# A graph-attention layer and a gated feed-forward layer on one core: the turned one-hots of the targets move from VectorE to ScalarE, made from single bytes

## The reference, cut to what matters

```python
x = x + gnn(layernorm(x), edges)
x = x + ffn(layernorm(x))

def gnn(x, edge_index, W, att_src, att_dst, bias):
    xp = (x @ W).reshape(n, 4, 64)
    a_src, a_dst = ...                      # a number per node and head
    alpha = leaky_relu(a_src[src] + a_dst[dst])
    ex = exp(alpha - segment_max(alpha, dst)[dst])
    w = ex / segment_sum(ex, dst)[dst]
    out = segment_sum(xp[src] * w[..., None], dst).reshape(n, 256) + bias
    return elu(out)

def ffn(x, ...):                            # 256 -> 1024 -> 256 with gelu,
    ...                                     # added for the half of the nodes with the largest router weight
```

## Time and profile before

| | us |
|---|---|
| timed: median of 3 runs (lowest, highest) | 2208.46 (2207.24, 2212.64) |
| profiled execution: span from its first to its last instruction | 2573.5 |
| of it: up to the first gathers, main stage, the rest | 132, 2350, 91.5 |

### The profile page before, as it was taken

How to read it: one execution, slowest core, us unless ns; L and a number is a source line. 1 busy time by engine, 2 the same in 40 slices (tenths; PEclk the granted TensorE clock), 3 DMA queues, 4 the chain that set the end, 5 groups by cost and what they waited for, 6 DMA issues and landing times.

```text
span 2573.5 us, 29095 instructions
## 1 busy us (share of the span) xinstructions
PE 1981.2 (77%) x9511; PEld 1633.8 (63%) x9512; DVE 1581.4 (61%) x3510; ACT 744.5 (29%) x1478; POOL 1554.5 (60%) x1626
## 2 busy tenths in 40 slices
PE   8935877877877877878778877877777777877787
PEld 6723666666666666666666666666666666666666
DVE  4555655665655655656656665666665665666576
ACT  4512222222322222322232232232232232223223
POOL 2366666666666666666666666666666666666630
PEclk9967988888888889889888888988988988889889
DMA  8844444444444444444444444444444444444447
GB/s 287 276 143 121 123 134 124 132 138 120 137 138 118 132 135 124 135 140 120 134 137 128 130 136 124 134 134 130 128 134 131 127 139 124 131 136 136 119 159 312
DMA packets 157137, 369.12 MB, mean 143 GB/s; under 512 B 46646, under 2 KB 73682, under 8 KB 155699
## 3 DMA queue, kind: packets, MB, share of 16 engines
q0 software_dynamic: 75088, 208.19, 30.1%
q1 hardware_dynamic: 74706, 145.62, 16.9%
q10 hardware_dynamic: 7184, 13.41, 1.4%
HBM read 328.20 MB, written 38.89 MB: 143 GB/s over the span
## 4 chain that ended last, share of the span: by engine, by line
POOL 38%; issue 23%; PE 19%; another core or an unknown queue 9%; DVE 3%; DMA 3%; ACT 2%; POOLq 1%; DVEq 0%; SPq 0%; ACTq 0%
POOL rows L692 38%; PE ag_ps L1057 7%; PE h_ps L1021 4%; PE ag_ps L934 3%; PE y_ps L1040 3%; DMA rows<-node_rows,ends 3%; POOLq L402 1%; DVE oh L1366 1%; DVE rows L1404 1%; ACT hT L808 1%; PE ag_ps L1128 0%; ACT L808 0%; PE ag_ps L1129 0%; ACT L812 0%
## 5 line engine op out<-in xcount | busy, mean ns | idle before, releaser
L692 POOL DMA_INDIRECT rows<-node_rows,ends x1563 | 1512.9, 968 | 850.6 <-issue 482.5
L1057 PE MATMUL ag_ps<-rows,oh 128*128 128x260 f32 x3518 | 845.9, 401 | 47.5 <-DVE rows L1404 34.8
L1021 PE MATMUL h_ps<-xnT,w1s 128*128 128x256 f32 x1568 | 534.0, 500 | 419.2 <-DVE zz L1385 227.1
L1057 PEld LDWEIGHTS ag_ps<-rows,oh 128*128 128x128 f32 x3518 | 716.7, 204 | 180.3 <-DVE rows L1404 37.8
L1021 PEld LDWEIGHTS h_ps<-xnT,w1s 128*128 128x128 f32 x1568 | 377.0, 250 | 517.9 <-DVE zz L1385 234.8
L1404 DVE TENSOR_TENSOR rows<-rows,xl_ps 128x512 f32<-128x512 f32 (+3 forms) x392 | 503.1, 1346 | 47.2 <-issue 26.5
L1385 DVE TENSOR_TENSOR zz<-rows,edge_dm 128x72 f32<-128x72 f32 x98 | 22.9, 233 | 695.0 <-DMA rows<-node_rows,ends 656.4
L1040 PE MATMUL y_ps<-w2s,hT 128*128 128x256 f32 x1568 | 368.0, 386 | 12.2 <-DVE oh L1366 9.2
L831 ACT COPY rows<-rows 128x780 f32<-128x780 f32 x97 | 81.6, 842 | 998.6 <-DMA rows<-node_rows,ends 998.6
L1040 PEld LDWEIGHTS y_ps<-w2s,hT 128*128 128x128 f32 x1568 | 301.7, 194 | 66.7 <-DVE oh L1366 16.6
L1366 DVE TENSOR_TENSOR oh<-xl_ps,dloc 128x2304 f32<-128x2304 f32 x98 | 249.0, 2541 | 0.0
(11 more groups left out here) (243 smaller groups left out, 1433.7 us busy)
## 6 DMA issues: line engine op xcount, KB each, us to landing
dbc<-dst SPq DMA_DIRECT2D x97, 576.0 KB
rows<-node_rows,ends POOLq DMA_INDIRECT x1563
selfr<-node_rows SPq DMA_DIRECT2D x98, 130.0 KB
base<-in_x SPq DMA_DIRECT2D x14, 896.0 KB, 7.1
base<-in_x SPq DMA_DIRECT2D x49, 256.0 KB
ffn_rows<-yb ACTq DMA_DIRECT2D x48, 256.0 KB
node_rows<-base SPq DMA_DIRECT2D x13, 910.0 KB, 5.7
base<-in_x_turned SPq DMA_DIRECT2D x14, 384.0 KB, 7.7
```

The costliest lines, as they stand in the source:

```text
L692: pool.indirect_dma_start(out=rows[:, b, t, :], out_offset=None, in_=table, in_offset=bass.IndirectOffsetOnAxis(ap=ends[:, b, t, 0:1], axi ...
L1021: last = nc.tensor.matmul(h_ps[:, m * PAIR:(m + 1) * PAIR], w1s[:, c, n * P:(n + 1) * P], xnT[:, c, :], start=(c == 0), stop=(c == DC - 1))
L1057: product = nc.tensor.matmul(ag_ps[b][:, 0:ROW], oh[:, b, t, :], rows[:, b, t, :], start=(t == 0), stop=False)
```

## The change

The 16-bit copy of the targets becomes a copy of their lowest bytes. The bytes go to a buffer of their own (`low`), and ScalarE makes the turned one-hot from them in two passes over 2304 elements: the square of the difference to the partition's low byte, then `relu(1 - 2 * square)` in place. It does so for the block after the next. VectorE no longer makes it, and TensorE's look-up waits for `dm_ok` as well, which VectorE's order had implied. The minimum with zero is taken of two tensors, the second a column of zeros that is read again for every element. Three loads of a register from the table now have their bounds tested on the chip (`min_val`, `max_val`); one of them runs in the main stage, `optional_landed`.

```diff
-        dst16_dram = nc.dram_tensor("dst16", (EP,), I16).ap()
+        dst8_dram = nc.dram_tensor("dst8", (EP,), U8).ap()
...
+        low = spare[:, 0:FLAT // 2].bitcast(U8).rearrange("p (a e) -> p a e", a=2)
+        low_id = spare[:, FLAT // 2:FLAT // 2 + 2]
+        minus_low = spare[:, FLAT // 2 + 2:FLAT // 2 + 4]
...
         def optional_landed(eng, w):
-            landed = eng.value_load(win[0:1, bass.ds(COLS * w + 7, 1)])
-            return nc.s_assert_within(landed, 16, 16 * (NW + 3), skip_runtime_bounds_check_because="a parity's first node block has one gather or more, each later one two at most")
+            return eng.value_load(win[0:1, bass.ds(COLS * w + 7, 1)], min_val=16, max_val=16 * (NW + 3))
...
             def load_targets(w, b, first):
                 if known(w, 2):
 
-                    sp.wait_ge(lk_ok, w - 1)
+                    wait_apart(sp, (apart_ok, w - 1))
                 flat = tiles_of(w) * P
-                sp.dma_start(dbc[:, b, 0:flat], dst16_dram[bass.ds(first * P, flat)].rearrange("(a e) -> a e", a=1).broadcast_to([P, flat])).then_inc(ld_dbc[b], 16)
+                sp.dma_start(low[:, b, 0:flat], dst8_dram[bass.ds(first * P, flat)].rearrange("(a e) -> a e", a=1).broadcast_to([P, flat])).then_inc(ld_dbc[b], 16)
...
+            def one_hots_turned(w, i, b):
+
+                flat = tiles_of(w) * P
+                act.wait_ge(ld_dbc[b], 16 * (i + 1))
+                if known(w, 2):
+                    act.wait_ge(lk_ok, w - 1)
+                nc.scalar.activation(oht[:, b, 0:flat], low[:, b, 0:flat], ACT.Square, bias=minus_low[:, b:b + 1]).then_inc(apart_ok, 1)
+                act.wait_ge(apart_ok, w + 1)
+                nc.scalar.activation(oht[:, b, 0:flat], oht[:, b, 0:flat], ACT.Relu, bias=1.0, scale=-2.0).then_inc(oht_ok, 1)
...
+                if not isinstance(w, int) or w + 2 < NW:
+                    one_hots_turned(w + 2, i + 1, b)
                 exponentials(w + 1, i + b, 1 - b)
...
                 pe.wait_ge(oht_ok, w + 1)
+                if known(w, 1):
+                    pe.wait_ge(dm_ok, w)
...
-                        pe.wait_ge(oht_ok, w + 3)
+                        pe.wait_ge(dm_ok, w + 2)
                     hidden(w - 3, 1 - b, i - 2 + b, (0,))
...
-            def one_hots_turned(w, i, b):
+            def local_targets(w, i, b):
 
                 n = tiles_of(w)
-                flat = n * P
-                dve.wait_ge(ld_dbc[b], 16 * (i + 1))
-                nc.vector.tensor_scalar(oht[:, b, 0:flat], dbc[:, b, 0:flat], node_id[:, bass.ds(w, 1)], None, ALU.is_equal).then_inc(oht_ok, 1)
                 dve.wait_ge(ld_ends[b], 16 * (i + 1))
...
-                nc.vector.tensor_scalar(zmin[:, :], zag[:, :], 0.0, None, ALU.min).then_inc(zmin_ok, 1)
+                nc.vector.tensor_tensor(zmin[:, :], zag[:, :], zero.broadcast_to([P, D]), ALU.min).then_inc(zmin_ok, 1)
```

More of the change, by code:

```diff
@@ L22 @@
 I16 = mybir.dt.int16
+U8 = mybir.dt.uint8
 ALU = mybir.AluOpType
@@ L163, in build @@
         xends = sb("xends", [P, 2], I32)
-        xdbc = sb("xdbc", [P, P], I16)
+        xdbc = sb("xdbc", [P, P], U8)
         xrow = sb("xrow", [P, ROW])
@@ L172, in build @@
         xdiff = sb("xdiff", [P, H])
-        column = sb("column", [P, 17])
-        rs1, rstd, sq, half, xloc, broken, broken_all, widest, in_order, first_f, length, nge, cur, kth, sixteen, always, first_block = (column[:, k:k + 1] for k in range(17))
+        column = sb("column", [P, 18])
+        rs1, rstd, sq, half, xloc, broken, broken_all, widest, in_order, first_f, length, nge, cur, kth, sixteen, always, first_block, zero = (column[:, k:k + 1] for k in range(18))
         xmax = sb("xmax", [P, H])
@@ L224, in build @@
         spare = sb("spare", [P, 6 * D])
+        low = spare[:, 0:FLAT // 2].bitcast(U8).rearrange("p (a e) -> p a e", a=2)
+        low_id = spare[:, FLAT // 2:FLAT // 2 + 2]
+        minus_low = spare[:, FLAT // 2 + 2:FLAT // 2 + 4]
+        assert FLAT // 2 + 4 <= 6 * D
         yin = []
@@ L261, in build @@
         key, sgn = key.bitcast(I32), sgn.bitcast(I32)
-        dst16 = dbc[:, 0, 0:EPP]
+        dst8 = dbc[:, 0, 0:EPP // 2].bitcast(U8)
+        lowest = dst_all[:, 0:EPP].bitcast(U8).rearrange("p (e k) -> p e k", k=4)[:, :, 0]
         xnT2 = dbc[:, 1, 0:4 * D].bitcast(F32).rearrange("p (a c q) -> p a c q", a=2, c=DC)
@@ L315, in build @@
          count_ok, before_ok, win_ok, gmax_ok, gall_ok, exact_ok, sdiff_ok, exself_ok, parts_ok,
-         pre) = sems(
+         pre, minus_ok, apart_ok) = sems(
             "pool_const col_ok const_ok ones_bf_ok d16_ok falls_ok earlier_ok blocks_ok block_ok b2_ok bias_step wext_mul_ok wext_ok stat_ok aggr_ok vareps_b rstd_b proj_ld trb_ok trc_ok xp_ok xpc_ok asd_ok "
-            "count_ok before_ok win_ok gmax_ok gall_ok exact_ok sdiff_ok exself_ok parts_ok pre")
+            "count_ok before_ok win_ok gmax_ok gall_ok exact_ok sdiff_ok exself_ok parts_ok pre minus_ok apart_ok")
         ld_ends, ld_dbc, ld_self, gath, gath_last = (sem2(n) for n in ("ld_ends", "ld_dbc", "ld_self", "gath", "gath_last"))
@@ L420, in for_extra @@
                 with eng.If(n > 0):
-                    before = entry(eng, w, 2, NW * EP // P)
+                    before = counted_before(eng, w, 2)
                     with eng.Fori(0, n) as j:
@@ L433, in if_exact @@
                     n = entry(eng, w, 3, EP // P)
-                    before = entry(eng, w, 4, NW * EP // P)
+                    before = counted_before(eng, w, 4)
                     with eng.If(n > 0):
@@ L482, in batch_io @@
                     sp.wait_ge(d16_ok, 1)
-                    sp.dma_start(dst16_dram.rearrange("(p e) -> p e", p=P), dst16).then_inc(d16_st, 16)
+                    sp.dma_start(dst8_dram.rearrange("(p e) -> p e", p=P), dst8).then_inc(d16_st, 16)
             def first_edge(w):
@@ L773, in batch_copies @@
                     act.wait_ge(dst_ld, 32)
-                    nc.scalar.copy(dst16, dst_all[:, 0:EPP]).then_inc(d16_ok, 1)
+                    nc.scalar.copy(dst8, lowest).then_inc(d16_ok, 1)
                 for t in range(BATCH):
@@ L888, in _ @@
             nc.scalar.preload_act_table_set(EXP_AND_LN)
+            act.wait_ge(minus_ok, 1)
+            for w in range(2):
+                one_hots_turned(w, 0, w)
             exponentials(0, 0, 0)
@@ L1345, in _ @@
             nc.vector.tensor_copy(parts[:, :, :, 2], left[:, :, :]).then_inc(parts_ok, 1)
+            nc.vector.tensor_copy(low_id, node_id[:, 0:2])
+            nc.vector.tensor_scalar(minus_low, node_id[:, 0:2], -1.0, None, ALU.mult).then_inc(minus_ok, 1)
             dve.wait_ge(exself_ok, 1)
@@ L1412, in weigh_self, with extra_tile @@
                     nc.vector.tensor_copy(selfr[:, b, D:ROW], e).then_inc(self_ok, 1)
-            def extra_tile(w, k):
+            def extra_tile(w, b, k):
                 dve.wait_ge(x_dbc, 16 * k + 16)
-                nc.vector.tensor_scalar(xoht[:, :], xdbc[:, :], node_id[:, bass.ds(w, 1)], None, ALU.is_equal).then_inc(x_oht, 1)
+                nc.vector.tensor_scalar(xoht[:, :], xdbc[:, :], low_id[:, b:b + 1], None, ALU.is_equal).then_inc(x_oht, 1)
                 dve.wait_ge(x_ends, 16 * k + 16)
@@ L1491, in window @@
                 if more:
-                    one_hots_turned(w + 1, i + b, 1 - b)
+                    local_targets(w + 1, i + b, 1 - b)
                 if not isinstance(w, int) or w < NW - 1:
@@ L1497, in window @@
                 weigh_self(w, i, b, alone)
-                for_extra(dve, dve_extras, w, lambda j, k: extra_tile(w, k))
+                for_extra(dve, dve_extras, w, lambda j, k: extra_tile(w, b, k))
                 if known(w, 1):
@@ L1512, in _ @@
             then(nc.vector.tensor_copy(iota_ps, iota_d[:, :]))
-            one_hots_turned(0, 0, 0)
+            then(nc.vector.memset(zero, 0.0))
+            local_targets(0, 0, 0)
             one_hots(0, 0)
```

4 lines of the change are left out of this document (3 added, 1 removed).

## The result

The changed kernel takes 2218.93 us in the median of 20 runs (2212.03 to 2225.45); the kernel before, in 20 runs beside them, takes 2209.93 us. The ratio is 1.0037, 95% interval 1.0029 to 1.0046: slower by 8.2 us, where 2190 us had been forecast.

What follows compares the result with a forecast made beforehand. GpSimd, making descriptors one after the other through the main stage, was taken to bound the kernel. The comparison's -18.6 us, all other terms at 0, took 2208.5 to 2190 us, range 2178 to 2217.

Steps and rivals of the forecast that it cites:

- the wait for TensorE's second layer: GpSimd's optional gathers wait for that layer; spare read as 0.2 to 0.4 us a block, cost put at 0.
- The bound: Main stage: GpSimd makes descriptors one after the other, a gather each 1.268 us, 20.3 us a block.
- the long waits: Idle time before gathers in the profiled run, 358.1 us together, taken to be absent from the timed run.
- The comparison: L1355 leaving VectorE: gathers beside it shorten by 21.6 us, its successors lengthen gathers by 3; -18.6 us.
- The minimum: L1449 on VectorE as two tensors: 0.10 us more a block, 9.8 us in all, in its slack: 0.
- The bounded load: Test of 213 ns between the gathers' landing and VectorE's first step: 0 to 20.9 us, taken as 0.
- the cover: In blocks with an optional gather, VectorE's wait for it hides the load's test; without this cover, 3.4 us.
- TensorE's loop: Rival: optional gathers wait for the second layer and swallow the gain; 2202 to 2215, say 2205 us; chance 0.20.
- TensorE's clock: Rival: longer idle time before the first layer's second part lowers TensorE's clock; 2224 us; chance 0.13.
- ScalarE's pair: Two one-hot passes ahead of copy L831: 4.2 us, at most 8.4, hidden in 6.8 us of idle time.
- The rule of the Trainium skill that I set aside: VectorE's two-port mode and GpSimd exclude each other for whole instructions; L1355 could cost 83.4 us, giving 2125; chance 0.01.

Runs made afterwards that it cites:

- e1: Kernel before with only the bounded loads added; ratio 1.0019 to the kernel before.
- e12: Kernel before with the bounded loads and the minimum of two tensors, without the one-hots on ScalarE; ratio 1.0058 to the kernel before.
- e3: Changed kernel with the bounded load moved ahead of VectorE's wait for the block's gathers; ratio 1.0009 to the kernel before.
- e5: Changed kernel with TensorE's second part of the first layer held back by an extra ScalarE copy; ratio 1.0033 to the kernel before.
- e13: Changed kernel with the intermediate sums in PSUM and the bounded load ahead of the wait for gathers; ratio 0.9964 to the kernel before.
- e11: Changed kernel with intermediate sums in PSUM, the load ahead of the wait, and TensorE held back by a ScalarE copy; ratio 0.9940 to the kernel before.
- e7: Changed kernel with VectorE's wait for ScalarE's exponential moved from behind L1477 to ahead of it; ratio 1.0039 to the kernel before.
- e9: Changed kernel with the intermediate sums of four VectorE instructions in PSUM instead of SBUF; ratio 0.9989 to the kernel before.
- e4: Changed kernel with the one-hots made on VectorE again by comparing bytes, ScalarE's two passes left out; ratio 1.0333 to the kernel before.

## Why the prediction was wrong

The three parts of the change, by e1, e12 and the change itself: loads +0.19%, minimum +0.39%, one-hots with all that goes with them -0.21% (the last is at the edge of what the runs can tell: the two intervals just touch). That is +4.2, +8.6 and -4.6 us of 2210, 8.2 together, the measured loss. Forecast and measurement lie 26.7 us apart (18.5 below and 8.2 above the kernel before). The prediction put three terms at nothing that make most of it: the minimum (8.6), the wait for TensorE's second layer (8.7), the bounded load (4.2).

**The bound.** GpSimd paces the kernel, and the timed run lacks the long waits: right. The span of 2218.6 against 2220.54 us, and a stretch that is 1563 x (0.946 + 0.302) = 1951 plus lengthening and waits (1951 + 20.8 + 21.1 = 1993 for 1992.5), say so.

**The comparison, -21.6 + 3 us: right in kind and nearly in size.** From e12 to the change the lengthening at the last two gathers falls by 16.0 us, that of all gathers by 17.0, for 18.6 forecast. Nothing new takes L1355's place there: inside L1384 and L1385, its successors, no gather begins that is then long, so the 3 us were not needed. That 21.6 less 3 comes so near is in part luck, since the 21.6 us came from a trace with other phases.

**The minimum, "in its slack: 0": the step that failed.** The prediction asked whether VectorE had idle time, and it had. It didn't ask which gather begins inside what the minimum pushes back. The 0.10 us were priced rightly and are paid in most blocks, 8.6 us, because L1477 ends 0.10 us later under a gather that ends 0.82 us behind it (77 or 78 twelfth gathers are held). Of the shown trace I had counted 8.1 us for all instructions of VectorE but L1355 and took that for their size; its long waits had spread the gathers' beginnings, and without those waits one place alone, the twelfth gather, has 7.6 (e1) to 15.6 us.

**The bounded load, 0 (up to 20.9):** 4.2 us. I had given 3.4 us as its price if the cover were gone. In the changed kernel it is paid through the same hold: e3 takes 6.3 us off the twelfth gather. That it is so in the old order is not shown.

**TensorE's loop, a rival at 0.20, at 0 in the sum:** it happened by half. From e12 to the change the waits rise by 8.5 us, half of the 16.0 gained, so that the one-hots alone would have made the kernel 0.2% faster and not 0.8%. The rival named the place: the waits ahead of the optional gathers and of each block's first, where GpSimd waits for the second layer, rise from 5.8 us to 14.5, all others together do not. Its sum was slightly off (0.30 + 14 x 1.25 is 17.8 us, not 17.9), so the spare that it read was 0.1 to 0.4 us.

**TensorE's clock, at 0.13:** the mechanism happened (0.949 to 0.928, 61 instead of 38 long parts). It was priced at 34 us; with the clock given back the waits fall by 4.5 us (e5) and 4.0 (e13 to e11), and the time by nothing that e5 can tell and by 0.24% from e13 to e11, with overlapping intervals.

**ScalarE's pair:** 4.3 us against 4.2 forecast, hidden.

**The rule of the Trainium skill that I set aside** (SBUF — State Buffer, section Who interferes with whom) gave 83 us for the comparison; the measured 16 us lie between it and nothing. That the later one waits until the whole instruction is done fits the held gathers, which end 0.12 or 0.82 us behind the end of VectorE's instruction. It does not say how many gathers meet one, and that is a matter of phase.

## What to carry to other kernels

Where GpSimd makes descriptors back to back, price an edit on VectorE by the gather that begins inside the instructions behind it, not by VectorE's idle time: the rows to read are those of one block, with the end of each long gather against the ends of VectorE's instructions. Moving such an instruction moved the hold to later gathers (e7); putting one of its two inputs into PSUM removed it (e9). And phases are read from a trace that is as long as the timed run: in one stretched by waits of its own, overlaps are counted at other places.

## What the runs showed of the hardware

An instruction of VectorE with two tensors in SBUF, running when a gather begins, lets that gather end 0.82 us behind its own end, whichever of these it is (L1472, L1474, L1477, L1480, L1507). The gathers so held began at least 0.03 us behind its start (L1477) and with more than 0.14 us of it left. With one of the tensors in PSUM no gather was held (L1429; the same four instructions in e9). Instructions with a single tensor in SBUF did hold gathers (the old minimum, 7 of 7 in e1; L1505, 40 of 66 in e9). The comparison of one tensor with a number per partition holds a gather that began before it as well, to 0.12 us behind its end (71 of 86 in e4). VectorE is slower in its turn: a comparison of bytes that begins 0.475 to 0.63 us into a gather takes 1.56 to 1.65 us instead of 1.41 (17 in e4).

VectorE compares bytes in 1443 ns where it compares 16-bit numbers in 859, for the same 2304 elements.
